# Identity products on TensorE ahead of two of its waits, in a one-core decoder layer

## The reference

```python
x = x + attn(layernorm(x))           # 32 query heads of 128, 8 key/value groups,
                                     # keys: 16 chosen cache blocks of 32, then the 128 new ones
x = x + xattn(layernorm(x), ctx)     # rmsnorm, 32 heads, position bias and mask, softmax
x = x + ffn(layernorm(x))            # gelu(x @ W1 + b1) @ W2, then + b2

def attn(x):
    q, k, v = x @ wq.T, x @ wk.T, x @ wv.T        # rope on q and k
    p = softmax(q @ k_full.T / sqrt(128))         # k_full: the chosen cache blocks, then k
    return (p @ v_full) @ wo.T
```

## Time and profile before

| what | value |
|---|---|
| median of 3 runs | 1894.92 us (1894.9 to 1896.09) |
| the profiled execution, its own time | 1894.83 us |
| its span, first to last instruction | 1893.0 us |
| TensorE busy | 1859.4 us, 98% |
| VectorE, ScalarE, GpSimd busy | 70%, 54%, 57% |
| mean granted clock of TensorE | 0.993 |

### The profile page before, as it was taken

How to read it: one execution, slowest core, us unless ns; L and a number is a source line. 1 busy time by engine, 2 the same in 40 slices (tenths; PEclk the granted TensorE clock), 3 DMA queues, 4 the chain that set the end, 5 groups by cost and what they waited for, 6 DMA issues and landing times.

```text
span 1893.0 us, 32031 instructions
## 1 busy us (share of the span) xinstructions
PE 1859.4 (98%) x9902; PEld 1598.2 (84%) x9902; DVE 1332.1 (70%) x2212; ACT 1030.4 (54%) x2265; POOL 1083.5 (57%) x861
## 2 busy tenths in 40 slices
PE   9899999999999999998999999999999999999998
PEld 6788888888888888876888888888888888888887
DVE  7688888888888888867666676666666766766132
ACT  3566666666666666655444444444444444445443
POOL 3788888888888888772443443333434434424643
PEclk9999999999999999998999999999999999999999
DMA  7555555555555555641222222222222222212332
GB/s 256 129 126 127 127 127 129 124 127 127 126 128 126 126 126 126 156 128 47 93 87 85 78 83 91 83 70 75 86 91 86 85 85 80 70 55 80 100 121 74
DMA packets 142282, 201.03 MB, mean 106 GB/s; under 512 B 29714, under 2 KB 67218, under 8 KB 141714
## 3 DMA queue, kind: packets, MB, share of 16 engines
q1 hardware_dynamic: 142226, 200.33, 38.0%
HBM read 98.25 MB, written 18.09 MB: 61 GB/s over the span
## 4 chain that ended last, share of the span: by engine, by line
PE 93%; DVE 3%; ACT 2%; issue 1%; SPq 1%; POOL 1%; DMA 0%; DVEq 0%; ACTq 0%
PE bank L1391 25%; PE bank L1392 25%; PE bank L1393 25%; PE bank L1471 11%; PE bank L1616 2%; PE bank L1617 2%; PE bank L1663 2%; PE bank L1664 2%; PE bank L1461 1%; DVE negmax L1012 1%; SPq L295 1%; DVE probT L1020 0%; DVE xacc L1031 0%; ACT prob L657 0%; PE bank L1412 0%
## 5 line engine op out<-in xcount | busy, mean ns | idle before, releaser
L490 POOL TENSOR_TENSOR pT_lo<-pT_lo,pT_hi 128x512 fp32r<-128x512 f32 x320 | 406.3, 1296 | 112.4 <-ACT pT_hi L598 112.4
L1031 DVE SCALAR_TENSOR_TENSOR xacc<-bank,rinv,xacc 128x512 f32<-128x512 f32 x504 | 364.0, 733 | 5.4 <-PE bank L1393 5.4
L657 ACT ACTIVATE prob<-bank,negmax 128x640 f32<-128x640 f32 x256 | 204.0, 797 | 253.1 <-DVE negmax L1012 252.2
L1020 DVE STREAM_TRANSPOSE probT<-prob 128x640 f32<-128x640 f32 x256 | 214.6, 838 | 108.7 <-ACT prob L657 108.7
L1012 DVE TENSOR_REDUCE negmax<-bank 128x1 f32<-128x640 f32 x256 | 207.3, 810 | 39.8 <-PE bank L1471 31.5
L473 POOL TENSOR_TENSOR xwo_lo<-xwo_raw,xwo_hi 128x512 fp32r<-128x512 f32 x32 | 41.5, 1298 | 268.4 <-ACT xwo_hi L598 268.4
L598 ACT ACTIVATE pT_hi<-pT_lo 128x512 fp32r<-128x512 f32 x320 | 185.6, 622 | 3.9 <-DMA pT_lo<-probT 3.9
L473 POOL TENSOR_TENSOR xwq_lo<-xwq_raw,xwq_hi 128x512 fp32r<-128x512 f32 x32 | 41.6, 1299 | 236.5 <-ACT xwq_hi L598 236.5
L1391 PE MATMUL bank<-wx_hi,cT_hi 128*128 128x256 f32 x512 | 142.2, 278 | 1.2 <-DVE xk L1140 1.2
L1393 PE MATMUL bank<-wx_hi,cT_lo 128*128 128x256 f32 x512 | 142.0, 277 | 0.0
L1392 PE MATMUL bank<-wx_lo,cT_hi 128*128 128x256 f32 x512 | 141.9, 277 | 0.0
(11 more groups left out here) (202 smaller groups left out, 5549.1 us busy)
## 6 DMA issues: line engine op xcount, KB each, us to landing
pT_lo<-probT SPq DMA_DIRECT2D x1024, 80.0 KB, 2.1
w_raw<-in_w SPq DMA_DIRECT2D x64, 256.0 KB, 2.8
xturned<-xturn SPq DMA_DIRECT2D x61, 256.0 KB, 2.0
xpraw<-xturned SPq DMA_DIRECT2D x244, 64.0 KB, 2.0
wx_raw<-in_wq SPq DMA_DIRECT2D x32, 256.0 KB, 2.6
wo_raw<-in_wo SPq DMA_DIRECT2D x32, 256.0 KB, 2.7
wx_raw<-in_xwv SPq DMA_DIRECT2D x16, 512.0 KB, 3.3
xwk_raw<-in_xwk SPq DMA_DIRECT2D x32, 256.0 KB, 2.8
```

What stands on the lines that cost most here:

```text
L490: g.tensor_tensor(tile, tile.bitcast(F32), four(pT_hi[:, j, :]), ALU.subtract).then_inc(a["pTlo"], 1)
L657: s.activation(prob[:, i % 2, :].rearrange("p (a t) -> p a t", a=2), S_bank[i % 2], ACT.Exp, bias=negmax[:, u % 2, i:i + 1], scale=1.0, ac ...
L1020: v.transpose(probT[:, u % 2, :, :, i * 32:(i + 1) * 32], prob[:, i % 2, :].rearrange("p (t j n) -> p j t n", j=4, n=32)).then_inc(a["turn ...
L1031: v.scalar_tensor_tensor(xacc[:, 4 * half + i, :], M, rinv[:, k, i:i + 1], xacc[:, 4 * half + i, :], ALU.mult, ALU.add).then_inc(sems["y"], 1)
```

## The change

Two calls of `spin` are added on TensorE. In turn 1 of the first attention 36 calls into bank 4 stand ahead of `V(0)`; bank 4 (`W_bank[0]`) has no other use before turn 2. Ahead of the second layernorm's first transpositions 24 calls into bank 6 stand behind the last `head_out` and ahead of the wait for `a["y"]`. No other instruction is changed, on any engine.

```diff
@@ -1555,6 +1555,8 @@
                 Q(0, 1)
                 S(1)
                 O(0)
+                if static and n == 1:
+                    spin(4, 36)
                 V(0)
                 Q(2, 3)
                 S(2)
@@ -1635,6 +1637,7 @@
             c_keys(0, 0, 0)
             for i in range(4):
                 head_out(n, n // 2, (n // 2) % 2, i, W_last[i])
+            spin(6, 24)
             pe.wait_ge(a["y"], LAST1)
             pe.wait_ge(c["vlo"], 2)
             second_transpose(0)
```

## The result

The changed kernel takes 1903.87 us (median of 5, 1902.82 to 1905.56) against 1894.92 (median of 5, 1894.47 to 1896.09): the ratio is 1.0051, with a 95% interval of 1.0038 to 1.0064, or 8.95 us. The forecast was 1900.2, and its range ended at 1902.6. The direction was right and the size was not. The profiled execution took 1903.87 us, its span 1902.1.

What follows compares the result with a forecast made beforehand. TensorE, busy 98% of the span, was taken as the bound, so delays last. +2.8 us at the first place and +2.5 at the layernorm gave +5.3 on 1894.92: 1900.2 us, own range 1899.6 to 1902.4, over all cases 1896.9 to 1902.6.

Steps and rivals of the forecast that it cites:

- The bound and the price of a call: TensorE bounds the kernel and keeps delays; a call is two matmuls, 0.223 us at the upper clock, 0.43 slow.
- The first place: 36 calls ahead of the first value product, turn 1 of the first attention: lateness that lasts, +2.8 us.
- the bounds of +2.6 and +4.3: First place: +2.6 us if TensorE's own lateness rules, +4.3 if the slow stretch comes again all the same.
- the slow stretch: Low-clock matmuls from `V(0)` to the third tile of values: 5.28 us becomes 3.64 behind the calls, 1.64 saved.
- the delay of `V(0)`: First value product: the 36 calls last 8.03 us, so it starts at 63.79 instead of 59.52, 4.27 us late.
- when the clock rises at the layernorm: At the 24 calls: rise taken at 865.3, between 864.4 and 866.1, so 5 slow matmuls and +2.5 us.
- Piece L: Second layernorm stretch, 855.46 to 869.60 us in the first profile of before; the forecast for this place was +2.5 us.
- back only at 869.95, as before: Second layernorm: if the clock returns only then, 27 slow matmuls instead of 5 and +4.8 us.
- The rival of the vanishing stretches: Low-clock stretches near 832 and 890 us vanish, each giving back about 1.7 us: 1898.5 or 1896.8; chance 0.29.
- Piece C: From the end of the layernorm piece to the second attention's loop of 4,200 matmuls; no term in the sum.
- nothing else moves: Rest of the kernel: no new instructions on other engines or queues, and they catch up on nothing TensorE needs.

Runs made afterwards that it cites:

- b1: The kernel before, unchanged, timed again against itself: 1894.19 us (12 executions), ratio 0.9999.
- b2: A further profile of the kernel before, unchanged: one execution, 1895.98 us.
- e2: The kernel before plus only the 24 calls ahead of the second layernorm's transpositions: 1898.94 us, ratio 1.0018.
- e7: The kernel before plus only 20 calls in the pause ahead of the last unit's third output projection: 1890.61 us, ratio 0.9982.
- a1: The changed kernel, unchanged, timed again against the kernel before: 1903.91 us (5 executions), ratio 1.0046.
- a2: A further profile of the changed kernel, unchanged: one execution, 1904.6 us.
- e1: The kernel before plus only the 36 calls ahead of the first value product: 1900.9 us against 1895.37, ratio 1.0032.
- e3: The changed kernel with 512-column calls, 9 instead of 36 and 6 instead of 24: 1902.39 us, ratio 1.0033 to the kernel before.
- e4: The kernel before plus 16 calls ahead of the first value product and 20 ahead of the third output projection: 1891.29 us against 1895.37, ratio 0.9977.
- e5: Calls in all TensorE pauses over 1 us, 19 of them ahead of the first value product: 1890.22 us against the kernel before's 1894.22, ratio 0.998.
- e6: The kernel before plus only 16 calls ahead of the first value product: 1893.53 us against 1894.22, ratio 0.9999.
- e8: The changed kernel with 72 calls instead of 36 at the first place: 1911.22 us against the kernel before's 1894.22, ratio 1.0085.

## Why the prediction fell short

**The bound and the price of a call: right.** 72 matmuls took 7.96 us where 8.03 was worked out, and the dense stretch handed every delay on.

**The first place: the mechanism right, the size too small.** I had +2.8 us. The 251st matmul comes at 76.2 us on the mean of the five profiles without calls there (before, b1, b2, e2, e7) and at 80.1 on that of the five with the 36 calls (after, a1, a2, e1, e3): +3.9. Against the three of before alone (77.1) the changed kernel's three (80.05) are +3.0, and in the first pair of profiles it was +1.7. All but the last lie inside the bounds of +2.6 and +4.3. That +3.0 is so near to +2.8 is partly luck: it is 4.9 for `V(0)` less 1.9 for the slow stretch, where the sum had 4.27 less 1.64. Two terms were mis-sized. One is the slow stretch that the calls give back: I took 1.64 us from the one profile. From `V(0)` to the 251st matmul the five without calls took 15.9 to 18.5 us, 17.1 on the mean, and those with the 36 calls 15.9 (e3 16.2): it is 1.1 us on the mean and 0.2 or nothing in two of five. The other is the delay of `V(0)`, 4.27 us in the sum and 5.0 on these means, since I took the room for the calls, 3.60 us, from one profile too. It was 1.4 to 4.6 us in the five. Nor do the calls always start early and quick: the low clock at about 50 us, which no call stands ahead of, falls into 48 to 56 us in other executions, and `V(0)` starts at 64.1 on the mean of the five and not at 63.8.

**The step that failed: when the clock rises at the layernorm.** I had it rise 3.8 us after work restarts, between two rows of other places, and so had 5 slow matmuls in the calls and +2.5 us. In the changed kernel work restarts at 863.32 and the clock rises at about 869.26, 5.9 us later, and in the six profiles with the 24 calls or their wide form this was 5.1 to 6.0; the two places it was taken from (2.9 and 4.6) did not carry over. The calls took 6.89 us where 5.87 was worked out, with 15 slow matmuls and not 5; the 16 transpositions behind them were as expected. Piece L is 14.0 to 14.1 us without calls at the layernorm and 17.5 to 17.9 in all six profiles with the 24 or their wide form, 17.8 in the change's three: +3.7. That is 1.2 us over the forecast for this place and 1.1 under the +4.8 of the case "back only at 869.95, as before". The Trainium skill's sentence on transpositions (TensorE: Matmul & The Clock Gate, PE-mode transpose), that the released clock doesn't engage for them, isn't borne out here: 16 of them took 1.91 us behind warm calls. Whether transpositions count as work that raises the clock, which is that sentence's reason, no run here tests.

**The rival of the vanishing stretches went the other way.** Piece C is 57.3 us on the mean of the three profiles of before and 58.3 in the three of the change: +1.0. The forecast had 0 for it and a rival that would give time back. The low clock at 890 us comes in one of three before, and in all three of the change (897 us in its first profile). In b1 and b2 it was missing. That it comes more often with the 24 calls, in five of six profiles that have them or their wide form, is seen; why is not shown. It also comes in e4 and e5, at about 885 us, and not in e7. The low clock at 832 us of the earlier trace rows is missing in b1 alone of the three profiles of before and the three of the change.

**The second attention: an effect of the execution, not of the change.** I said nothing else moves. The 3.6 us that the first pair of profiles shows there is chance: 718.2 to 720.5 us in the kernel before, 719.5 to 721.8 in the changed one. On the mean the change's three are 1.4 us slower, which three profiles each can't tell from nothing.

The sum by the measured pieces is 3.0 to 3.9 + 3.7 + 1.0 = 7.7 to 8.6, and 0 to 1.4 for the loop. That meets the 8.95 and 9.2 us timed. The table leaves out two pieces, which are +0.4 us (from the 251st matmul to L, where b1 lacks the low clock at 832 us) and +0.2 (behind the loop) between the means of three profiles. So of the 3.65 us that the forecast fell short, the late rise at the layernorm is 1.2, the only part that all profiles show alike; the rest is piece C and what differs from one execution to the next. In the first pair of profiles it was shared out otherwise: the first place 1.1 under its forecast, the layernorm 1.2 over, and 3.5 in the loop, by chance.

**Where the change's aim lies.** The low clock at the layernorm comes from the pause of 4.72 us ahead of the third output projection: it begins inside the pause in all eleven profiles that leave the pause empty, and it is absent in the three that fill it. Calls behind that pause take 6.89 us and give back only 3.2 of them (the wait of 0.85 us and the quicker matmuls behind them). Twenty calls inside it cost nothing and take piece L from 14.1 to 10.8 us. At the first place 16 calls gain nothing that can be measured. The pause there is not the same in each execution: they left 0.99 us of it in e4 and outlasted it by 0.5 in e6. The fastest versions are e7, e5 and e4, 1890.2 to 1891.3 us, about 4 us under the kernel before; e7, with its 20 calls alone, is the simplest of them.

## What to carry to other kernels

Work that only keeps the clock up must stand ahead of the pause's end on the engine's own program, and must be shorter than the pause: measure the pause, divide by the price of a call (here 4.72 us by 0.223), and stop one short. Measure it in several executions: the pause at the layernorm was 4.7 us in each profile that left it empty, the one ahead of the first value product 1.4 to 4.6. If TensorE is the bound, every call beyond the pause is paid one to one (e8: 36 more cost about 8 us, 36 x 0.223), and one that runs at the low clock costs nearly double (0.43 us). Before a stretch of low clock in one profile is entered into a sum as a saving, look at a second profile of the same program: of three here, none had its low clock in the same places at the start.

## What the runs showed of the hardware

The second attention's matmuls of 256 columns run at one of two distances, about 0.113 and 0.118 us, in groups, at a granted clock of 1.00 throughout. The share of each changes between executions of one and the same program, and with it the time of 4,200 matmuls, 718.2 to 720.5 us. In the changed kernel it was 719.5 to 721.8. The 3,750 matmuls of the first attention's dense part took 744.0 us in nearly every profile. What chooses the pace is open; no run was made for it.

A float32 product of the identity shows as two matmuls in the trace. Each of the two took 0.407 us with 512 columns, 9% less than four of 128 columns (0.446).

The clock fell inside the pause of 4.7 us at the layernorm. It stayed low for 10.2 us in the five profiles without calls there, and for 6.8 us in the six with the 24 calls or their wide form behind the pause. With 20 calls inside the pause it did not fall.
